# Expert inputs and outputs moved by indirect DMA through memory, and a reordered front of the attention stage, in a four-layer fp32 kernel

## What is computed

```python
# layer 2, T = 625, NE = 8, top 2, cap = int(1.2 * 625 / 8) = 93
probs = softmax(xf @ gate_w.T + gate_b)            # xf = layernorm(x)
topw, topi = top_k(probs, 2); w_te = topw scattered to [T, NE]
wm = where(routed, w_te, -1.0)
sel_w, sel_idx = top_k(wm.T, cap)                  # each expert's 93 best tokens
sel_w = maximum(sel_w, 0.0)
xg = xf[sel_idx]                                   # [8, 93, 512]
h = gelu(xg @ w1 + b1)                             # w1: [8, 512, 2048]
out = h @ w2 + b2                                  # w2: [8, 2048, 512]
x = x + zeros.at[sel_idx].add(out * sel_w)
# layer 4, 8 groups x 16 heads = 128 heads, 100 pooled keys per group
w = silu(k @ aw1 + aw1_b) @ aw2 + aw2_b            # pooling weights, softmax both ways
kc, vc = pooled keys and values                    # [100, 8, 128] each
att = softmax(q . kc / sqrt(128)); z = att . vc    # per head
h1 = silu(l2norm(z) * g1 @ wz_w1 + wz_b1)          # z: [625, 16384], wz_w1: [16384, 1024]
x = x + silu(l2norm(h1) * g2 @ wz_w2 + wz_b2)
```

## Time and profile before

| What | us |
|---|---|
| median of three runs | 2200.32 |
| the profiled execution, own time | 2200.64 |
| its span in the trace | 2198.6 |
| PE busy in it | 2122.9 |
| DVE busy | 1509.0 |
| ACT busy | 1127.4 |
| POOL busy | 855.7 |

### The profile page before, as it was taken

How to read it: one execution, slowest core, us unless ns; L and a number is a source line. 1 busy time by engine, 2 the same in 40 slices (tenths; PEclk the granted TensorE clock), 3 DMA queues, 4 the chain that set the end, 5 groups by cost and what they waited for, 6 DMA issues and landing times.

```text
span 2198.6 us, 36208 instructions
## 1 busy us (share of the span) xinstructions
PE 2122.9 (97%) x13402; PEld 1975.6 (90%) x13402; DVE 1509.0 (69%) x3183; ACT 1127.4 (51%) x3011; POOL 855.7 (39%) x688
## 2 busy tenths in 40 slices
PE   8888899999879999999999999999999999999998
PEld 7766566668669999999999999999999999999997
DVE  8736788864346777776677777677767667777776
ACT  4534556642435555554555554455555445555554
POOL 0000000000234555554455555455555545555551
PEclk9888999999979999999999999999999999999999
DMA  6000788870121112221111222111121211112110
GB/s 211 1 20 4 248 277 279 278 259 5 43 66 62 62 62 78 88 79 64 62 62 62 88 78 81 62 62 63 62 99 67 81 62 62 62 63 100 63 43 24
DMA packets 85688, 197.42 MB, mean 90 GB/s; under 512 B 5938, under 2 KB 10322, under 8 KB 85512
## 3 DMA queue, kind: packets, MB, share of 16 engines
q1 hardware_dynamic: 85512, 195.12, 26.1%
HBM read 193.75 MB, written 1.35 MB: 89 GB/s over the span
## 4 chain that ended last, share of the span: by engine, by line
PE 89%; ACT 4%; DVE 4%; issue 1%; DMA 1%; POOL 0%; SPq 0%; DVEq 0%; POOLq 0%; ACTq 0%
PE PS L54 80%; PE PS L53 5%; PE PS L57 4%; ACT HW L88 1%; ACT GT L88 1%; ACT HS L88 0%; DMA X<-in_x 0%; DVE JU L66 0%; DMA RAW<-in_L_ffn_w 0%; DVE OHs L68 0%; ACT EE L88 0%; POOL SM L60 0%; DVE SM L107 0%; DVE OHd L69 0%; DVE M L75 0%
## 5 line engine op out<-in xcount | busy, mean ns | idle before, releaser
L54 PE MATMUL PS<-ZH,WS 128*128 128x314 f32 x4096 | 946.8, 312 | 0.0
L54 PEld LDWEIGHTS PS<-ZH,WS 128*128 128x128 f32 x4096 | 691.9, 189 | 0.0
L54 PE MATMUL PS<-ZL,WS 128*128 128x314 f32 x2048 | 625.7, 306 | 0.0
L60 DVE TENSOR_TENSOR ACC<-ACC,PS 128x314 f32<-128x314 f32 x1008 | 476.4, 477 | 197.0 <-PE PS L54 187.1
L54 PEld LDWEIGHTS PS<-ZL,WS 128*128 128x128 f32 x2048 | 387.8, 189 | 0.0
L60 POOL TENSOR_TENSOR WS<-RAW,WS 128x512 fp32r<-128x512 f32 x256 | 327.4, 1300 | 109.3 <-ACT WS L88 109.2
L60 POOL TENSOR_TENSOR ML<-MF,MH 128x400 fp32r<-128x400 f32 x128 | 134.2, 1049 | 413.2 <-ACT MH L88 413.1
L60 POOL TENSOR_TENSOR ZS<-ZS,ZQ 128x628 f32<-128x628 f32 x128 | 198.7, 1552 | 234.9 <-ACT ZQ L88 234.9
L88 ACT ACTIVATE ZH<-PS,g1T 128x628 fp32r<-128x628 f32 x128 | 100.6, 786 | 321.4 <-PE PS L54 321.4
L88 ACT ACTIVATE EE<-EE,SM 125x100 f32<-125x100 f32 x640 | 233.4, 375 | 13.8 <-DVE SM L68 11.0
L88 ACT ACTIVATE MF<-PS 128x400 f32<-128x400 f32 x128 | 64.6, 505 | 319.6 <-PE PS L53 319.6
(11 more groups left out here) (336 smaller groups left out, 3738.1 us busy)
## 6 DMA issues: line engine op xcount, KB each, us to landing
RAW<-in_L_ffn_wz_w SPq DMA_DIRECT2D x66, 1024.0 KB, 6.1
RAW<-in_L_ffn_w SPq DMA_DIRECT2D x64, 1024.0 KB, 7.8
RAW<-in_L_ffn_Wq_w SPq DMA_DIRECT2D x32, 1024.0 KB, 5.3
CB<-c_rows SPq DMA_DIRECT2D x32, 195.3 KB
RAW<-in_L_gnn_W SPq DMA_DIRECT2D x4, 1024.0 KB, 8.7
RAW<-in_L_ffn_Wkv_w SPq DMA_DIRECT2D x4, 1024.0 KB, 5.3
RAW<-in_L_ffn_Wk_T SPq DMA_DIRECT2D x2, 1024.0 KB, 5.2
WB<-w_rows SPq DMA_DIRECT2D x6, 305.2 KB
```

The source lines that it names most:

```text
L54: return self.q.matmul(o, l, r, start=start, stop=stop)
L60: return Nothing() if self.q is None else self.q.tensor_tensor(out=o, in0=a, in1=b, op=op)
```

## The change

The MoE stage no longer picks and returns rows by products, for seven of eight experts. ACT's normalized rows `MU` are written to memory (`x_rows`, ten DMAs of SP). `WSP` gets the token's number as two more columns, so that the small product gives, beside the weight, the number of the token in each slot (`IX`); POOL then brings the 94 rows of the next expert with one indirect DMA (`XR`), and PE transposes `XR` instead of `OT`. The split copies `XFH` and `XFL` and the ten products for each expert go. `dispatch(e + 1)` on PE stands behind `up(e, 2)` and is five small products.

On the way back the scaled outputs of experts 0 to 6 are written to memory (`y_rows`, two DMAs each, row 0 is zero). Each token is in at most two experts, so `places()` works out for each token the lowest and the highest row among them (`IL`, `IH`), ten indirect DMAs of 125 rows bring them (`YL`, `YH`), and DVE adds them to `X` once each, during expert 7. Only expert 7 is still returned by products. SP's `load_row(2)` moves behind the third weight load and `sp_pool` behind the ninth.

In the attention stage the loop begins at i = 3. The first four heads' `m_` stand ahead of it between the keys; their query weights have four buffers instead of two and are split earlier; `values(2)` and `values(3)` and the second `bias_rows` stand behind the first burst; burst j stands at i = 4j + 3; the first four heads run one step earlier, with their transposes in other PSUM banks. Wq blocks are due one earlier in the order of loads. At the very end the last adds are shared between POOL (three tiles) and DVE (two), with five buffers.

```diff
@@ loads
-        for _, kind, b in sorted([(4 * b - 1, 0, b) for b in range(32)] + [(2 * r + 6, 1, r) for r in range(64)]):
+        for _, kind, b in sorted([(4 * b - 2, 0, b) for b in range(32)] + [(2 * r + 6, 1, r) for r in range(64)]):
@@ sp_moe
+            def outputs(e):
+                q.wait_ge(*os_hi.of(e))
+                for lo, hi in ((0, 80), (80, CS)):
+                    q.dma(yrow[1 + CS * e + lo:1 + CS * e + hi, :], OS[lo:hi, e % 2, :]).then_inc(s_yw[e % 2], 16)
...
             load_b2(0)
+            for t in range(T5):
+                q.wait_ge(*mu_done.of(t))
+                for lo, hi in ((0, 120), (120, 125)):
+                    q.dma(xrow[P * t + lo:P * t + hi, :], MU[lo:hi, t, :]).then_inc(s_rows, 16)
...
-            load_row(2)
-            sp_pool(q)
             for m in range(64):
                 q.wait_ge(*w_used.of(m))
                 load(q, N_MOE + 8 + m)
+                if m == 2:
+                    load_row(2)
+                if m == 8:
+                    sp_pool(q)
...
+                if m % 8 == 7 and m // 8 < NE - 1:
+                    outputs(m // 8)
@@ g_moe
+            for e in range(NE):
+                k = e % 2
+                q.wait_ge(*sw_v.of(e, "index"))
+                if e >= 2:
+                    q.wait_ge(*xg_t.of(e - 2))
+                q.gather(XR[:, k, :], xrow, IX[k][:, :]).then_inc(s_xr[k], 16)
+            q.wait_ge(*code_v.of("low"))
+            q.wait_ge(s_yw[0], 32 * 3)
+            q.wait_ge(s_yw[1], 32 * 3)
+            for t in range(T5):
+                q.gather(YL[:, t, :], yrow[0:1 + 6 * CS, :], IL[:, t:t + 1]).then_inc(s_yl, 16)
+            q.wait_ge(*code_v.of("high"))
+            q.wait_ge(s_yw[0], 32 * 4)
+            for t in range(T5):
+                q.gather(YH[:, t, :], yrow, IH[:, t:t + 1]).then_inc(s_yh, 16)
@@ v_moe
+            def back(Y, s, name):
+                q.wait_ge(s, 16 * T5)
+                for t in range(T5):
+                    if name == "high":
+                        q.wait_ge(*x2_done.of("low", t))
+                    q.tt(X[:, t, :], X[:, t, :], Y[:, t, :], ALU.add).then_inc(*x2_done.up(name, t))
...
                 if e == NE - 1:
                     v_counts(q)
+                    back(YH, s_yh, "high")
                 scale(e)
@@ pe_moe
             def dispatch(e):
-                k = e % 2
                 q.wait_ge(*rank_v.of(e, "po"))
...
+                q.wait_ge(*free[3])
                 q.wait_ge(*gate_v.of("wsl"))
                 for t in range(T5):
+                    i = q.mm(PS[0:CS, 3, 0:4], PO2[:, e % 2, t, :], WSP[:, t, e, :], t == 0, t == 4)
...
             def gathered_T(e):
-                q.wait_ge(*ga_done.of(e))
+                q.wait_ge(s_xr[e % 2], 16 * (e // 2 + 1))
@@ ffn1
-        LAST = NH + 7
+        FIRST, LAST = 3, NH + 7
+        def head_of(i, lag):
+            h = i - lag + 1
+            if not 0 <= h < 4:
+                h = i - lag
+                if not 4 <= h < NH:
+                    return None
+            return h
...
         def burst_of(i):
-            return i // 4 - 1 if i % 4 == 0 and 4 <= i <= NH else None
+            return i // 4 if i % 4 == 3 and i < NH else None
```

More of the change, by code:

```diff
@@ L120, in select, with gather @@
         return self.q.affine_select(out=o, in_=o, compare_op=op, fill=fill, base=0, pattern=pattern, channel_multiplier=mult)
+    def gather(self, dst, src, index):
+        if self.q is None:
+            return Nothing()
+        return self.q.indirect_dma_start(out=dst, out_offset=None, in_=src, in_offset=bass.IndirectOffsetOnAxis(ap=index, axis=0))
     def dma(self, dst, src):
@@ L1105, in a_moe @@
                 rows(t)
-            for t in range(T5):
-                q.wait_ge(*xfh_done.of(t, "u"))
-                q.act(XFH[:, t, :], MU[:, t, :], ACT.Copy).then_inc(*xfh_done.up(t))
             def rank_row(e):
@@ L1370, in v_moe @@
             rank_end(0)
-            for t in range(2, T5):
-                rest(t)
             diagonal(1)
@@ L1395, in v_moe @@
                     rank_end(e + 2)
-                if e + 1 < NE:
-                    dispatch(e + 1)
+                if e == NE - 1:
+                    back(YL, s_yl, "low")
                 weights(n + 8)
@@ L1992, in g_ffn1 @@
             g_power(q, r5, r5, hp[0:P, 0:5], o_g, "norm")
+            for t in range(3):
+                q.wait_ge(*o_a.of(t))
+                q.tt(X[:, t, :], X[:, t, :], OT1[:, t, :], ALU.add).then_inc(*x4_g.up(t))
         def a_ffn1(q):
@@ L2062, in bias_rows @@
                     q.wait_ge(s_cr, 16)
-                q.act(CR[:, :, :], four(PS[0:16, 5 + b, 0:4 * L]), ACT.Copy).then_inc(*kc_hi.up("rows", b))
+                q.act(CR[:, :, :], four(PS[0:16, 6 - 2 * b, 0:4 * L]), ACT.Copy).then_inc(*kc_hi.up("rows", b))
             keys(0)
-            values(2)
             def z_(h):
@@ L2538, in last @@
                     i.then_inc(*o_mm.up(t))
[L2540 to L2543 removed]
+            m_(0)
+            m_(1)
+            keys(4)
+            m_(2)
+            keys(5)
+            m_(3)
+            keys(6)
+            keys(7)
+            for i in range(FIRST, LAST + 1):
+                todo = wz_todo(i)
+                h = head_of(i, 6)
+                if h is not None:
+                    z_(h)
+                if early(i):
+                    attT(head_of(i, 5))
                 if burst_of(i) is not None:
                     burst(burst_of(i))
[L2546 to L2555 removed]
+                if i + 1 < NH:
+                    m_(i + 1)
+                if i == 3:
+                    values(2)
+                if i == 6:
+                    bias_rows(1)
+                    free[4] = kc_hi.of("rows", 1)
                 if i == LAST:
@@ L2561, in pe_ffn1 @@
                     wz(*a)
-                if 0 <= i - 5 < NH:
-                    attT(i - 5)
+                h = head_of(i, 5)
+                if h is not None and not early(i):
+                    attT(h)
+                if i == 4:
+                    values(3)
                 for a in todo[4:6]:
```

452 lines of the change are left out of this document (256 added, 196 removed).

## The result

The changed kernel takes 2222.09 us (median of four runs, 2219.94 to 2223.31), the kernel before 2200.31: a ratio of 1.0099, with a 95% interval of 1.0085 to 1.0113. It is slower by 22 us, where I had forecast 46 us less.

The account below looks back on a forecast made before the run. PE was taken as the bound, busy 97%, with DMA close behind and binding the changed MoE stage. MoE 35.3, attention front 10.9 and end 0.3 gave 46.5 us off 2200.6: 2154, range 2136 to 2172.

Parts of the forecast that it names:

- the new steps off the path: MoE stage: a gather takes 5 us, some 10 us are hidden; net 0 at the start, returns 0, up to 7.
- The slower rival: PE waits at the transposes of XR in every expert, needing a gather of 19 us or more; about 2224, chance 0.04.
- the gathers or the front are dearer: Rival: gathers of 12 us instead of 5, dearer returns or a smaller front gain; 2166 to 2194, chance 0.17.
- What DMA can deliver: MoE stage: the busiest DMA engines need 29.2 us per expert against PE's 25.7; stage 222.7 us, 35.3 less.
- The 28.8 us: MoE stage: DMA time of an expert if WB takes 2.6 us by the rule on partition counts, instead of 29.2.
- the first expert's stall is in this difference: Expert 0: the stall's removal counts within the 35.3 us, as its first load is issued at 218.8 instead of 225.2.
- The start ahead of it: Ahead of expert 0: 4.3 us of dispatch and copies go, about 5 come; net 0, between -1 and +4.
- The returns: Expert 7: YH gathers start some 8 us in, 2.6 us available for each; cost 0, up to 7 us.
- The attention front: Fourth key to second burst: burst starts 5.2 us earlier, plus 2.3 by clock and 3.4 behind; 10.9 less, between 7 and 14.
- The end: Last adds of the kernel: with five buffers and POOL's help the last add starts 0.3 us sooner.
- the one of a late `YH`: Sign of being wrong: YH arrives late ahead of expert 7's OT; no size given.
- those for being right: Experts 2 to 5 about 29 us, HW waiting some 3, first load at 219, XR in 4 to 6, second burst at 602.

Follow-up runs that it names:

- plain_pool_rows: Changed kernel with XR brought by an ordinary POOL DMA of the first 94 rows instead of an indirect one; 2194.64 us, one execution.
- early_gather: Changed kernel with the next expert's small product and index at the head of the expert, from expert 1 on; 2209.36 us, ratio 1.0040.
- early_rows_on_16: early_gather with bias and rank rows loaded as two DMAs each; 2187.87 us, ratio 0.9931.
- start_rows: Changed kernel with expert 1's rank row and ranks ahead of the first XGH and XGL, and WB loaded ahead of the loop's first weight load; 2214.24 us.
- rows_on_16: Changed kernel with each bias row loaded as two DMAs (80 and 14 partitions) and each rank row as two (120 and 5); 2210.12 us, ratio 1.0041.
- index_behind_split: Changed kernel with DVE's index of the next expert moved from ahead of a weight split to behind it; 2217.76 us, one execution.
- front_only: Kernel before with only the attention half of the change, the MoE stage left as it was; 2188.39 us, ratio 0.9946.
- all_moved: Changed kernel with the edits of early_gather, rows_on_16 and start_rows, later YL gathers, earlier expert 6 outputs, expert 1's index at expert 0's head; 2176.17 us.
- products_mended: front_only with the edit of rows_on_16, the third rank row behind the loop's first weight load, small loads behind the ninth; 2181.87 us, ratio 0.9908.

## Why the prediction was wrong, step by step

From the 46.5 us less that I forecast to the 22.3 more of the profiled execution it is 68.8 us: 54.3 in the MoE stage (35.3 less was forecast, it is 19.0 more), 11.7 in the returns, 5.6 at the start, and 2.8 the other way in the attention stage and the graph convolution ahead of it.

**The step that failed** is "the new steps off the path", where I took 5 us for a gather, "nearer the small one, because its size is". It takes 7.6 with an empty queue and 10.6 to 15.3 in the experts. The upper bound that I had written down, 14.4, was the right end: the gather's price is not in its bytes. plain_pool_rows shows that more than half of it is the indirection. Two more terms of the same step were off. The index was to be there 12 us into an expert; it is there at 14.1, behind the steps that stand ahead of it in DVE's list. And a gather from POOL was to be free of DVE; DVE's split behind the index holds it 2.1 us.

**The slower rival** named the right mechanism and place. I asked for a gather of 19 us, having counted 12 us from the index to the transposes (the step itself has "some 10"). In expert 2 there are 22.4 - 14.6 = 7.8 from the gather's issue on, and behind the wait PE's clock is down (0.58 in the stretch above), which I had left out: 12.9 - 7.8 = 5.1 of wait and 2 of clock. The rival above it in my list ("the gathers or the front are dearer") had 12 us for a gather, nearly the measured size, and put 2 us for each of seven experts on some 29, where experts 2 to 5 took 33.3 to 37.6: 2182 for 2222.

**What DMA can deliver**: the bound is real but was hidden under the wait for `XR`. early_gather uncovers it at 31.5 us an expert, not 29.2, and early_rows_on_16 shows that the bias and rank rows are part of it (2.7). Of the 2.3 that I was short, the gather explains 0.9 (1.4 instead of 0.5); the rest is open. The 28.8 us that I worked out beside it don't come out of their terms: 21.6 + 3.9 + 2.6 + 1.0 are 29.1, and the forecast did not use them.

**The first expert**: "the first expert's stall is in this difference" did not hold. The first weight load did start earlier (227.0, 5.4 us into the expert instead of 9.1; I had 2.7), but `WB` now stood behind three of them; start_rows and rows_on_16 each take part of the stall away. The start ahead of it was to cost -1 to +4 and seems to cost 5.6, with a wait of PE of 6.5 at the first `XR`. But 2.1 of that are there already at the products `SM` x `ones`, 37 us ahead, which stand at 179.12 and 181.23; in index_behind_split, with the changed program up to there, they stand at 178.85. Counted from them it is 3.5, within what I gave.

**The returns** were taken at 0, up to 7, and cost 11.7: `YH` is issued at 484.5 to 491.0, since expert 6's output landed only then, and lands by 506.9. I had 2.6 us for each gather and put the first 8 us into expert 7; the first was issued 11.7 us into it, and they landed 3.5 us apart on the mean (492.7 to 506.9).

**The attention front** was 10.9, within 7 to 14: front_only gives 12.4, the trace 13.0 up to the second burst, 5.9 ahead of the first burst (5.2 forecast) and 7.1 behind its start (5.7). This holds for executions in which the front runs at full clock; the two others of front_only gain only 2 us, which I had not foreseen. **The end** is 0.4 for 0.3 predicted. Expert 7 has PE's 25.7.

Of my signs, the one for the slower rival (PE waiting at `XR`) and the one of a late `YH` were there, and POOL over 3 us. Of those for being right one was nearly there (ACT's `HW` waits for `RAW` six times, 15.7 us in all); the times of the experts, of the first load, of `XR` and of the second burst (670.8) were not.

## What to carry to other kernels

A transfer that replaces products is free only if what it needs is ready early: add up the list of the engine that makes its index, not only its own steps, and put the index at the head of the stage. Here the loads became the bound once PE was relieved: splitting two rows into two DMAs each took 2.7 us off an expert, and holding back loads that nobody needed yet took 8.2 off the last wait. And `WB`, moved behind three loads, was late: DVE waited 12.0 us for it.

## What the runs showed of the hardware that I had not expected

An indirect DMA of 94 rows of 2 KB from POOL takes 7.6 us to landing alone, an ordinary one of the same bytes 2.9. Beside a stream of 1 MiB loads it is 12.7 to 15.3 against 5.7 to 7.7 (the last six of each kernel). One more in each expert costs 1.4 us, by one execution. In all_moved ten gathers of 125 rows, issued every 1.5 to 2.3 us beside loads, land one in 2.8 us; with six of the loads held back the last lands 8.7 us sooner.

POOL's part of such a gather is 1.48 us and grows to 3.58 where DVE starts two subtractions of SBUF operands (2.35 us) just ahead.

A stretch of the attention stage's front ran at 1.2 GHz in front_only's trace and at 2.4 in that of products_mended, with the same instructions and the same waits of PE ahead of it in the last 30 us (2.0, 1.5, 1.3 and 1.0 us the longest). The executions of front_only alone fall into two groups 10 us apart. What decides it stays open; no run here varied it.
